# Logits of a graph layer taken from two PSUM banks at once, 1024 columns at a time, through one place instead of two

## The reference

```python
Q = Xa @ W1
K = Xa @ W3
logits = Q @ W2 @ K.T / TAU
idx = jnp.argsort(-logits, axis=1)
vals = jnp.take_along_axis(logits, idx, axis=1)
csum = jnp.cumsum(jax.nn.softmax(vals, axis=1), axis=1)
k_i = jnp.sum(csum < P_NUC, axis=1) + 1
...
masked = jnp.where(keep, logits, -jnp.inf)
return jax.nn.softmax(masked, axis=1)
...
for s in range(STEPS):
    A = _adj_from_feats(Xa, W1, W2, W3)
    Xf = Rf @ Xf
    Xb = Rb @ Xb
    Xa = A @ Xa
    Z = Z + (Xf @ U1[s] + Xb @ U2[s] + Xa @ U3[s])
```

## Time and profile before

| what | value |
|---|---|
| median of 3 runs | 3918.45 us (3916.76 to 3919.89) |
| the profiled execution, whole | 3916.46 us |
| its span, first to last instruction | 3914.6 us |
| mean granted TensorE clock | 0.890 of full speed |
| PE busy | 2999.4 us, 77% |
| DVE busy | 3537.1 us, 90% |
| ACT busy | 3135.8 us, 80% |

### The profile page before, as it was taken

The page is one execution under the profiler, slowest core; times in us unless marked ns, Lnnn a source line. Parts: engine busy times, 40 slices in busy tenths (PEclk is TensorE's granted clock), DMA queues, the critical chain, the costliest instruction groups (busy, mean ns, idle before and its releaser), DMA issues. The chain is left out here.

```text
span 3914.6 us, 41324 instructions
## 1 busy us (share of the span) xinstructions
PE 2999.4 (77%) x14148; PEld 2085.4 (53%) x14148; DVE 3537.1 (90%) x4635; ACT 3135.8 (80%) x4153; POOL 366.9 (9%) x456
## 2 busy tenths in 40 slices
PE   6468778687877768748878778696878766699999
PEld 4356656466656656414544435353444545477777
DVE  6999999999999998499999999999999967577776
ACT  6999999999999997399999999999999912233333
POOL 3000000000000000000000000000000026244433
PEclk8688889898988989868989889898989887899999
DMA  2112121222222121211111110110111034222221
GB/s 89 53 52 85 59 90 52 74 77 66 77 68 90 44 82 62 108 54 44 45 34 46 35 45 29 43 45 29 45 36 51 20 102 131 100 101 93 94 100 49
DMA packets 108900, 254.24 MB, mean 65 GB/s; under 512 B 11984, under 2 KB 47888, under 8 KB 105360
## 3 DMA queue, kind: packets, MB, share of 16 engines
q1 hardware_dynamic: 82768, 217.76, 17.3%
q10 hardware_dynamic: 25920, 33.83, 2.4%
HBM read 217.47 MB, written 34.08 MB: 64 GB/s over the span
## 5 line engine op out<-in xcount | busy, mean ns | idle before, releaser
L677 DVE SCALAR_TENSOR_TENSOR s_dump<-s_rows,s_mid 128x3327 bf16<-128x3327 f32 x608 | 2238.1, 3681 | 1.0 <-issue 0.6
L626 ACT ACTIVATE s_adump<-s_rows,s_mid 128x3327 bf16<-128x3327 f32 (+1 forms) x324 | 995.0, 3071 | 10.5
L630 ACT ACTIVATE s_adump<-s_rows,s_mid 128x3327 bf16<-128x3327 f32 (+1 forms) x324 | 991.2, 3059 | 6.5 <-ACT s_sx_out L525 3.2
L878 PE MATMUL bank<-x,s_slab 128*128 128x512 f32 x1352 | 623.4, 605 | 0.0
L922 PE MATMUL bank<-hb,s_wT 128*128 128x256 f32 x1352 | 360.6, 412 | 142.9 <-ACT s_wT L503 142.4
L922 PE MATMUL bank<-xab,s_wT 128*128 128x256 f32 x1352 | 350.8, 404 | 119.1 <-ACT s_wT L503 118.8
L878 PEld LDWEIGHTS bank<-x,s_slab 128*128 128x128 f32 x1352 | 261.8, 195 | 279.7 <-issue 269.1
L855 PE MATMUL bank<-kh,qs 128*128 128x512 f16 (+1 forms) x364 | 142.7, 392 | 305.8 <-DVE s_rows L656 294.8
L1312 ACT ACTIVATE e_wh<-bank 128x512 f16<-128x512 f32 (+1 forms) x182 | 102.4, 565 | 335.1 <-PE bank L1412 335.0
L922 PEld LDWEIGHTS bank<-hb,s_wT 128*128 128x128 f32 x1352 | 260.2, 203 | 200.3 <-ACT s_wT L503 106.6
L911 PE MATMUL bank<-ident,s_rows 128*128 128x128 f32 x1352 | 227.4, 295 | 162.8 <-DVE s_rows L731 153.0
(11 more groups left out here) (175 smaller groups left out, 4744.9 us busy)
## 6 DMA issues: line engine op xcount, KB each, us to landing
s_slab<-adjT_dram SPq DMA_DIRECT2D x104, 448.0 KB, 3.9
e_adj<-adjR_dram SPq DMA_DIRECT2D x26, 1664.0 KB, 6.9
s_slab<-adjT_dram SPq DMA_DIRECT2D x104, 384.0 KB, 3.7
strip<-adjR_dram SPq DMA_DIRECT2D x52, 448.0 KB, 3.5
strip<-adjR_dram SPq DMA_DIRECT2D x52, 384.0 KB, 3.3
su_d<-s_su_out ACTq DMA_DIRECT2D x26, 256.0 KB, 2.0
zu_d<-s_zu_out ACTq DMA_DIRECT2D x26, 256.0 KB, 2.1
sx_d<-s_sx_out ACTq DMA_DIRECT2D x26, 256.0 KB, 2.0
```

The costliest lines, as they stand in the source:

```text
L626: nc.scalar.activation(adump[:], row(g, r), ACT.Sign, bias=st(mid, g, 2), accum_out=cnt[:]).then_inc(S["a_eval"], 1)
L630: nc.scalar.activation(adump[:], row(g, r), ACT.Relu, bias=st(mid, g, 2), accum_out=gap[:]).then_inc(S["a_eval"], 1)
L677: nc.vector.scalar_tensor_tensor(out=dump[:], in0=row(g, r), scalar=st(mid, g, r), in1=row(g, r), op0=ALU.is_gt, op1=ALU.mult, accum_out=s ...
L878: ins = nc.tensor.matmul(acc, slab[:, i % NSLAB, j - PIECES[p], :], s_op[:, j, 0:SN], start=False, stop=(j == NT - 1))
```

## The change

The two banks become one tensor of 1024 columns. A chunk is now up to 1024 columns wide, so a tile has 4 chunks (3 of 1024 and one of 255) instead of 7. PE writes a chunk with four matmuls instead of two, in the same order of columns, and signals once. DVE takes 1024 columns in one instruction. As both banks are used for one chunk, there is one place instead of two, and PE waits for the take of the chunk just before (n - 1) instead of the one before that (n - 2). The counts in `due` follow: 12 chunks over the same 27 beats in place of 21, and 8 in place of 14 in the last loads.

```diff
-        psum = [ctx.enter_context(nc.psum_tensor(f"bank{b}", [P, CH], F32)) for b in range(8)]
+        wide_psum = ctx.enter_context(nc.psum_tensor("banks0and1", [P, 2, CH], F32))
+        psum = [wide_psum[:, b, :] for b in range(2)] + [... for b in range(2, 8)]
...
-    psL, psT, psA, psS = psum[0:2], psum[2:4], psum[4:6], psum[6:8]
+    psL = env["wide_psum"][:].rearrange("p b n -> p (b n)")
+    psT, psA, psS = psum[2:4], psum[4:6], psum[6:8]
...
-                nc.vector.tensor_scalar(rows[:, home(g, r), ch * CH:ch * CH + w], psL[n % 2][:, 0:w], 1.0, None, ALU.mult, ALU.max,
+                nc.vector.tensor_scalar(rows[:, home(g, r), ch * WIDE:ch * WIDE + w], psL[:, 0:w], 1.0, None, ALU.mult, ALU.max,
...
-                if n >= 2:
-                    pe.wait_ge(S["lg_free"], n - 1)
-                cols = slice(ch * CH, ch * CH + w)
+                if n >= 1:
+                    pe.wait_ge(S["lg_free"], n)
                 lhs = qs[:, t * P:(t + 1) * P]
-                nc.tensor.matmul(psL[n % 2][:, 0:w], lhs, kh2[:, cols], start=True, stop=False)
-                nc.tensor.matmul(psL[n % 2][:, 0:w], lhs, kl2[:, cols], start=False, stop=True).then_inc(S["lg_done"], 1)
+                for o in range(ch * WIDE, min(ch * WIDE + WIDE, N), CH):
+                    cols = slice(o, min(o + CH, N))
+                    part = psL[:, o - ch * WIDE:cols.stop - ch * WIDE]
+                    nc.tensor.matmul(part, lhs, kh2[:, cols], start=True, stop=False)
+                    ins = nc.tensor.matmul(part, lhs, kl2[:, cols], start=False, stop=True)
+                ins.then_inc(S["lg_done"], 1)
...
-                        for n in due(b, 34 - 9 * loads, 34, NCH * loads):
-                            logits(3 * NCH * (g + 1) + n)
+                        for n in due(b, 34 - 9 * loads, 34, NWIDE * loads):
+                            logits(3 * NWIDE * (g + 1) + n)
```

More of the change, by code:

```diff
@@ L25 @@
 NCH = -(-N // CH)
+WIDE = 2 * CH
+NWIDE = -(-N // WIDE)
 NPAIR = NT // 2
@@ L79, in program @@
         x1_d = scratch("x1_d", (P, NT, D))
-        psum = [ctx.enter_context(nc.psum_tensor(f"bank{b}", [P, CH], F32)) for b in range(8)]
+        wide_psum = ctx.enter_context(nc.psum_tensor("banks0and1", [P, 2, CH], F32))
+        psum = [wide_psum[:, b, :] for b in range(2)] + [ctx.enter_context(nc.psum_tensor(f"bank{b}", [P, CH], F32)) for b in range(2, 8)]
         def sb_in(stack):
@@ L370, in layer_step @@
         xa_out = sb(tag + "xa_out", [P, RXA, D], F32)
-        mx = sb(tag + "mx", [P, 6, NCH], F32)
+        mx = sb(tag + "mx", [P, 6, NWIDE], F32)
         nb, Z, target, mid, hit, mass, kept, rk = (
@@ L648, in take @@
             def take(n):
-                l, ch = divmod(n, NCH)
+                l, ch = divmod(n, NWIDE)
                 g, r = LOADS[l]
-                w = chunk_width(ch)
+                w = min(WIDE, N - ch * WIDE)
                 if ch == 0 and g >= 2:
@@ L660, in highest @@
                 g, r = LOADS[l]
-                dve.wait_ge(S["lg_free"], NCH * (l + 1))
+                dve.wait_ge(S["lg_free"], NWIDE * (l + 1))
                 nc.vector.tensor_reduce(st(nb, g, r), mx[:, home(g, r)], AX.X, ALU.max, negate=True).then_inc(S["nb_ready"], 1)
@@ L775, in _ @@
                 column_rates()
-            for n in range(3 * NCH):
+            for n in range(3 * NWIDE):
                 take(n)
-                if n % NCH == NCH - 1:
-                    highest(n // NCH)
+                if n % NWIDE == NWIDE - 1:
+                    highest(n // NWIDE)
             def between(g, b):
@@ L800, in between @@
                     start = 35 - 9 * loads
[L801 to L805, removed]
+                    for n in due(b - 1, start, 35, NWIDE * loads):
+                        if n % NWIDE == NWIDE - 1:
+                            highest(3 * (g + 1) + n // NWIDE)
+                    for n in due(b, start, 35, NWIDE * loads):
+                        take(3 * NWIDE * (g + 1) + n)
             for g in range(LAST):
```

## The result

The changed kernel takes 3958.65 us in the median of four executions (3957.1 to 3960.69), the kernel before 3919.17 us beside it. The ratio is 1.0102, with a 95% interval of 1.0084 to 1.0119: slower by 1.0%, some 39 us. I had forecast slower, at 3946 us with an upper end of 3955. The direction and the main cause held, the size did not. The profiled execution took 3960.69 us, with a span of 3958.9.

The account below looks back on a forecast made before the run. Openings bound by a PE-DVE chain, step 0 groups by DVE, step 1 groups by PE. 3916.5 + 15.7 + 15.8 - 2.1 - 0.5 = 3945.4 us, taken as 3946; own range 3942 to 3949, widened to 3933 to 3955.

Parts of the forecast that it names:

- What bounds the kernel now: Openings: a chain of PE and DVE; step 0 groups: DVE, ACT close; step 1 groups: DVE and ACT wait for PE.
- A take: In the groups, a DVE take of 1024 columns lasts about 1.12 us, 0.08 less than two takes of 512.
- the dear take: A take over two banks costs as much as two, 1.20 us; 2.6 us are missing, giving 3948.
- The openings: With one place PE and DVE take turns at 1.2 GHz; each step's opening lasts 32.0 us, +15.7 and +15.8.
- The groups of step 0: DVE saves 5.5 us on takes but keeps only ACT's slack ahead of the last group: -2.1 us.
- The sum: Profiled 3916.5 us plus 15.7 plus 15.8 minus 2.1 minus 0.5 gives 3945.4; as a median 3947.4, taken as 3946.
- The groups of step 1: Take savings vanish into DVE's wait for PE's wide chunk; -0.5 us remains, extra matmul pairs bounded at +-3.0 us.
- The rise of the clock: Rival: TensorE's clock rises inside both openings, adding 20.9 us instead of 31.5; 3935 us, chance 0.20.
- Longer loops: Rival: step 1's loops lengthen through chunk pairs ahead of transposes or PE waiting a beat for DVE; 3952 us, chance 0.10.
- The ring: Rival: in step 1 ACT and PE stop holding each other at transposes, returning 20.3 us; chance 0.05.
- its own mark of 7.8 us: Smallest difference from no change that a measurement of this kernel can tell: 0.2%, 7.8 us.
- The second place was not worthless: Rival, here denied: the openings' second place was worth nothing, so only the takes count; 3914 us, chance 0.03.

Follow-up runs that it names:

- the first and the third experiment: Changed kernel with the opening as before (512 columns, two places): 3921.14 us; changed kernel with two places of 1024 columns in the opening: 3917.52 us.
- the third trace of the changed kernel: The changed kernel itself, unaltered, timed and traced a third time on another chip: 3950.44 us, ratio 1.0081.
- the second trace: The changed kernel itself, unaltered, timed and traced again: 3951.2 us, ratio 1.0083.
- the narrow groups: Changed kernel with its opening kept and the groups as before (512 columns, two places): 3954.08 us, ratio 1.0086.
- the fed groups: Changed kernel with idle matmuls of 512 columns where PE waits for ACT in step 1's groups: 3951.12 us, ratio 1.0079.
- the 70 groups counted above: Third to seventh groups of step 1 in fourteen traces (kernel before, changed one, twelve of the experiments): 11 last over 175 us, 59 last 174.0 or 174.1.

## Why the prediction was wrong in size

**What bounds the kernel now.** Right for the openings and step 1. In step 0 DVE was not the bound with ACT "close behind". ACT has no wait at all from the third group on and is the bound, and DVE was already tied to it at line 755.

**A take.** 1.14 us measured, 1.12 forecast. Right; the dear take of 1.20 did not come.

**The openings.** 31.7 and 32.5 us measured, 32.0 forecast for both, at the clock that I had chosen: the granted clock was 0.51 and 0.50. The Trainium skill, "TensorE: Matmul & The Clock Gate", section "A second HAM failure mode: psum-queue depth-cycling", tells of a kernel in which short idle times between groups of matmuls made the clock swing between its levels. In these openings it did not swing but stayed down, and only with the gap filled was it up. The second place is worth 32 us here, by the first and the third experiment. The Trainium skill, same page, section "HAM oscillation — how this bites in real kernels", tells of a matmul kernel in which double-buffering in PSUM gave no further gain; here it was worth those 32 us.

**The groups of step 0.** The step that failed first in time. The sum had -2.1, the profiled execution shows +1.0. I read the slack at the exponential that DVE asks for at line 666 and did not look for another place where DVE waits for ACT. There was one, `low_parts`, with 0.8 us of waits in the groups of the kernel before: no slack at all. What DVE saved went into waits there (5.2 us), and ACT, which never waited, went on at its own pace. The +1.0 itself is no more than spread: the third trace of the changed kernel has 1368.4 us for these groups, the second 1371.6. The term should have been 0.

**The groups of step 1.** The step that failed most. -0.5 with bounds of +-3.0 against +10.2. The reasoning on the beats held: DVE's waits merged into one and the transpose of beat 18 was not later. What I priced at nothing, without a reason, was the clock in the groups, and the bounds came from the pairs of matmuls alone. In the rows of the kernel before, the ring of ACT and PE ran at 1.00 behind PE's waits, and I took 174.0 us for a property of the code. It holds only where the clock is up while PE makes the transposes that ACT waits for next. A group in which it is down some 26 us in costs 1.4 to 1.8 us, and 3.0 or 3.1 in the two where it stayed down from 19 to 29 us in (177.0 and 177.1). A fall that is over by 22 us costs nothing. One costly fall stood in the kernel before as well (the group of 175.4), and I did not ask why. That this is the cause, and not the wide chunks, is shown by the narrow groups that are long too, by the fed groups from the third on that are not, and by the 70 groups counted above. In the first group, and in the second one of the fed kernel (175.1), what lengthened them stays open. Why the wide openings bring more costly falls is not shown. A pause of the same length ahead of step 1 does not do it (1380.5 us).

**The number.** The span came out 15.4 us above the sum: 10.7 of them in the groups of step 1, 3.1 in those of step 0, 1.2 in the stretch between the steps, which I had at nothing and which lasts 196.1 to 198.7 us in the traces of kernels that leave it alone, and 0.4 in the openings and the rest. I also took 3946 where the sum gave 3947.4 as a median, for no reason that I named. Against nine later executions, 3949.3 to 3955.0, the forecast of 3946 was some 5 us low; 2.1 of them are the term of step 0, 1 to 3 the long groups of step 1 (1381.1 and 1383.2 us against 1380.1). The first result lies some 7 us above their middle. Its trace has two long groups more than the two later ones and a last group longer by 3.4 us, in which the clock fell twice; together they are those 7 us against the second trace. Why its four executions all came out so stays open.

**The rivals.** The rise of the clock did not happen. "Longer loops" happened, but by the clock and not by the pairs of chunks ahead of transposes or a wait of a beat, which is what I had named. The ring did not open: in no trace did a full group of step 1 behind the first two fall under 174.0 us. With its own mark of 7.8 us the prediction should also have asked 21 us of this rival, or 11 with the clock up, and not 24 and 13; it changes no branch. The second place was not worthless, and a take over two banks was not dear.

## What to carry to other kernels

A wide take over two banks saves about 0.07 us each, and it pays only where its engine is the one that is waited for and nothing else is tied to it; look for every wait of that engine, however small, before counting the saving. Giving up the second place cost nothing that could be measured in the groups, where a chunk is handed over every two or three beats, and 16 us in each opening, where producer and consumer have nothing else to do; take the second place from banks that are idle there. Where a group's length hangs on a ring of waits, look at the granted clock inside it before calling the length a constant, and at which place it falls: the same fall cost nothing ahead of a wait that took it up, and 1.4 us or more behind it.

## What the hardware showed that was not expected

In openings in which PE worked 1.9 us and stood 1.3 us, the granted clock stayed at 0.50 for 32 us. Idle work of three matmuls in each gap made the opening 7.5 us shorter, though PE had more to do. In the groups of step 1 a wait of PE of 2.69 us was followed by 1.2 GHz in some groups (the one at 2209 us of the changed kernel) and by 2.4 GHz in others (the one at 2172 us of the kernel before), with the same instructions ahead of it. Which it is differed between the traces of one kernel. How much of the spread between executions comes from it is not shown: each kernel was traced once, and in the trace of the kernel with only its openings as before, 2.9 us of the 4.4 by which its span is longer lie behind the groups of step 1 (878.3 us against 875.4).
